# Attention on one core: the weighted values of two steps of the keys issued together

## The reference

```python
attn = jnp.einsum('bhqd,bhkd->bhqk', query, key) / scale
attn = jax.nn.softmax(attn, axis=-1)
out = jnp.einsum('bhqk,bhkd->bhqd', attn, value)
```

## Time and profile before

| | |
|---|---|
| Timed runs, median of 3 | 3951.06 us (3947.47 to 3952.72) |
| Profiled execution, its time by the profiler (its span; the page gives no other) | 4004.2 us |
| Mean granted TensorE clock in it | 0.952 |
| TensorE, VectorE, ScalarE, GpSimd busy in it | 3682.7, 3108.8, 2340.3, 646.8 us |
| Stage that the change touches | 459 to 3400 us of the span |

### The profile page before, as it was taken

One profiled execution on the slowest core, in us unless ns is written; L12 is line 12 of the kernel. 1 busy time (PEld: TensorE's weight loads), 2 busy tenths in 40 slices (PEclk: granted clock), 3 DMA queues, 4 the chain that ended last, 5 costly groups with the idle time before them and its releaser, 6 DMA issues. The chain is left out here.

```text
span 4004.2 us, 70540 instructions
## 1 busy us (share of the span) xinstructions
PE 3682.7 (92%) x19328; PEld 1342.4 (34%) x19328; DVE 3108.8 (78%) x5336; ACT 2340.3 (58%) x4484; POOL 646.8 (16%) x838
## 2 busy tenths in 40 slices
PE   6775999999999999999999999999999999575888
PEld 3432233323323322333233323322332332464555
DVE  6887988888888888888888888888888885575222
ACT  2322477777767776777677767767777777100111
POOL 5554000000000000000000000000000000355554
PEclk9887799999999999999999999999999999776999
DMA  5556202020202111120202020202112000466442
GB/s 152 171 161 170 42 22 50 21 54 13 55 13 57 26 44 38 30 44 24 45 27 54 12 55 12 54 13 59 29 38 44 23 15 15 137 198 190 146 141 85
DMA packets 268209, 258.28 MB, mean 65 GB/s; under 512 B 59140, under 2 KB 225581, under 8 KB 267601
## 3 DMA queue, kind: packets, MB, share of 16 engines
q1 hardware_dynamic: 252496, 224.42, 22.0%
q0 software_dynamic: 15360, 29.50, 2.6%
HBM read 159.56 MB, written 103.49 MB: 66 GB/s over the span
## 5 line engine op out<-in xcount | busy, mean ns | idle before, releaser
L813 DVE TENSOR_REDUCE max_parts<-ps_m 128x1 f32<-128x512 f32 x4096 | 2546.0, 683 | 394.2 <-PE ps_m L698 392.3
L791 ACT ACTIVATE probs<-ps_s 128x512 f32<-128x512 f32 x4096 | 2129.3, 603 | 811.9 <-PE ps_s L718 811.7
L698 PE MATMUL ps_m<-keys,queries 96*128 96x512 bf16 x4096 | 1580.7, 386 | 33.3 <-DMA queries<-split_q 32.9
L718 PE MATMUL ps_s<-queries,keys 99*128 99x512 bf16 x4096 | 1564.4, 383 | 31.5 <-issue 25.4
L733 PE MATMUL ps_o<-probs,vals 128*32 128x512 f32 x8192 | 1094.7, 606 | 0.3 <-ACT weighted L780 0.2
L718 PEld LDWEIGHTS ps_s<-queries,keys 99*128 99x128 bf16 x4096 | 397.1, 97 | 1301.8 <-issue 819.7
L698 PEld LDWEIGHTS ps_m<-keys,queries 96*128 96x128 bf16 x4096 | 400.0, 98 | 474.2 <-DVE max_parts L813 92.5
L659 POOL TENSOR_TENSOR heads_out<-weighted,recip_rows 128x512 f32<-128x512 f32 x64 | 81.3, 1270 | 2103.1 <-DMA recip_rows<-recip_rows_dram 2103.1
L733 PEld LDWEIGHTS ps_o<-probs,vals 128*32 128x32 f32 x8192 | 161.4, 108 | 371.3 <-issue 356.5
L1509 DVE TENSOR_TENSOR hidden<-ps_u,silu 128x320 f32<-128x320 f32 x64 | 30.9, 491 | 178.3 <-PE ps_u L1445 131.3
L647 POOL TENSOR_TENSOR neg_split<-neg_max,zeros_b 128x16 bf16<-128x16 f32 x64 | 14.1, 220 | 771.3 <-DVE neg_max L821 771.3
(11 more groups left out here) (103 smaller groups left out, 1931.7 us busy)
## 6 DMA issues: line engine op xcount, KB each, us to landing
queries<-split_q SPq DMA_DIRECT2D x384, 64.0 KB
rows<-rows_c SPq DMA_DIRECT2D x16, 1032.0 KB, 6.4
vext<-val SPq DMA_DIRECT2D x64, 256.0 KB, 3.6
vals<-vext SPq DMA_DIRECT2D x32, 512.0 KB
recip_rows<-recip_rows_dram SPq DMA_DIRECT2D x64, 256.0 KB
att<-heads_out SPq DMA_DIRECT2D x64, 256.0 KB, 2.7
split_q<-parts SPq DMA_DIRECT2D x96, 128.0 KB
split_k<-parts SPq DMA_DIRECT2D x96, 128.0 KB
```

The costliest lines, as they stand in the source:

```text
L698: pe.matmul(ps_m[bank][:], queries[0:SROWS, par, qt, j, t * P:(t + 1) * P], keys[0:SROWS, par, j, c * 512:(c + 1) * 512], start=True, stop ...
L718: pe.matmul(ps_s[n % BANKS][:], keys[0:MROWS, par, j, k * P:(k + 1) * P], queries[0:MROWS, par, qt, j, :], start=True, stop=True).then_inc ...
L791: act.activation(probs[:, n % RING, :], ps_s[n % BANKS][:], ACT.Exp, scale=SCALE).then_inc(probs_ok[n % BANKS], 1)
L813: dve.tensor_reduce(max_parts[:, lu % 2, g:g + 1], ps_m[bank][:], AX.X, ALU.max).then_inc(maxima_ok[bank], 1)
```

## The change

In `step_of`, the weighted values are no longer issued after every group for the group before, but after every second group (those of even number) for the two groups before: sixteen matmul instructions in a row in place of eight. After group 0 of a step those are the last two groups of the step before, and at the end of the last step two groups are left to weigh instead of one. `weigh`, its waits, the banks and the rings are the same, as is the code of the other engines.

```diff
-                        if n:
-                            weigh(step, n - QUAD)
-                        elif not first:
-                            weigh(step - 1, TILES - QUAD)
+                        if n // QUAD % 2 == 0:
+                            for back in (2 * QUAD, QUAD):
+                                if n:
+                                    weigh(step, n - back)
+                                elif not first:
+                                    weigh(step - 1, TILES - back)
...
-                weigh(STEPS - 1, TILES - QUAD)
+                for back in (2 * QUAD, QUAD):
+                    weigh(STEPS - 1, TILES - back)
```

## The result

The changed kernel takes 4095.99 us (median of 4; 4094.93 to 4098.22) against 3951.89 us (median of 4). The ratio is 1.036, 95% interval 1.035 to 1.038: slower, by 144 us where 182 were forecast (4133 us, range 4075 to 4185).

What follows compares the result with a forecast made beforehand. TensorE was taken to set the pace in attention, VectorE 0.36 us behind per group; units +176, last groups +5 and one more group at the end +1 gave +182 on the 3951 us median: 4133 us, range 4075 to 4185.

Steps and rivals of the forecast that it cites:

- The direction and the mechanism: Attention: slower, as eight tiles in a row outrun VectorE with three ps_m banks; 0.49 us of waiting added per pair.
- from the fourth tile of a run on: Attention runs: the forecast is wrong if TensorE isn't held by reductions from this tile on.
- The saved passage: Between short matmuls and weighted values in attention: one passage in and back less per pair of groups saves 0.175 us.
- Rival A: Attention: drains are the bound and banks don't bind, 5.515 us a pair, 3863 us in all; chance 0.05.
- A pair: Two groups in attention: 6.00 us against 5.69, with a burst of 1.91 us; loses 0.31 us.
- The once-in-a-unit work: Attention, per 16 groups: neg_max +0.44 us, reciprocal +0.16, ps_o copy +0.03 come out; the transposition's 0.29 is swallowed.
- A unit: Sixteen groups in attention: 48.6 us against 45.81, so +2.8 us on each of 62.75 units, +176.
- The last groups: Last 20 groups, without ps_m: TensorE waits for ScalarE; 5.26 us a pair against 4.80, +5 us.
- Rival B: Attention: new waits bring the clock to the lower level a tenth of the time, +256 us, 4389; chance 0.06.
- The row DMAs: DMAs of the maxima in attention: keep their window, costed at nothing; +60 us if they waited in every unit.
- C: Burst in attention: the sixteen matmuls don't run on, 2.00 us instead of 1.91, +45, 4178 us; chance 0.12.
- D: Attention: hidden VectorE work stays hidden or banks free sooner, 0.6 us less a unit, 0.05 a pair, 4070; chance 0.14.

Runs made afterwards that it cites:

- the short reductions: Changed kernel with VectorE reducing only 256 of 512 columns of each ps_m: 3931.2 us, ratio 0.982; the kernel before with the same: 3981.3 us, 0.995.
- the shifted version: Changed kernel with neg_max and the reciprocals moved to the second half of a run: 4117.5 us, ratio 1.042 to the kernel before.
- mended four banks: Changed kernel with four ps_m banks, bank wait and transposition moved to the second scores, ps_o copy moved into the burst: ratio 0.986 to the kernel before.

## Why the prediction was right, and what it had too large

- **The direction and the mechanism**: right. The run of eight waits for reductions from the fifth tile on, tile 7 starts at 3.78 us, VectorE idles 1.09 us in each burst (about 1.2 said). Shown by the short reductions and by two, three and four banks. The sign "from the fourth tile of a run on" in the prediction (and in the first expectation) was a slip against its own sum: the fourth tile has 0.15 us to spare, the fifth is held by 0.02 us and each later one by 0.16.
- **The saved passage**: its size was too small by the terms, and came out right in the total by luck. Rival A's premise, that no bank is late, was wrong. With the wait taken away a pair takes 5.513 us in the loop, A's 5.515; but the burst of sixteen is 0.05 us shorter than A has it, and ScalarE, "ahead of its turn" in the prediction, holds the last scores of each run by about as much. Where ScalarE doesn't, a pair takes 5.45, so one passage less is worth 0.24 us and not 0.175. The trace agrees in so far with the rule that a change of tiling mode drains TensorE (the Trainium skill, TensorEngine Tiling (Array Packing), Key Properties), that a passage in and out has this price; it doesn't show what the engine does in it.
- **A pair**: 5.96 us, not 6.00. The term that was too large is the burst of sixteen, 1.86 and not 1.91 us. The second and third set follow each other closer than the first two, as this timeline of one burst's weight loads and matmuls shows, 0.46 and then 0.43:

```profile
2041.30 1.92 PE L720 MATMUL ps_o<-probs,vals 128*32 128x512 f32 x16
2041.76 0.13 PEld L720 LDWEIGHTS ps_o<-probs,vals 128*32 128x32 f32 x4 [0.30 <-issue]
2042.19 0.13 PEld L720 LDWEIGHTS ps_o<-probs,vals 128*32 128x32 f32 x4 [0.30 <-issue]
2043.16 0.39 PE L705 MATMUL ps_s<-queries,keys 99*128 99x512 bf16 x1
```

  Eight pairs a unit: 0.32 us too much, 20 us over the stage.
- **The once-in-a-unit work**: neg_max +0.35 (0.44 said), reciprocals +0.10 (0.16), copy +0.04 (0.03), transposition swallowed. 0.13 us a unit too much, 8 us in all. The kinds were right, as the shifted version shows.
- **A unit**: 48.18 against 48.6; the difference to the kernel before is 2.37 us, not 2.82. On 62.75 units that is 28 us of the 39 by which the sum for attention (+182, measured +143.5) was too large. This is the term of the sum that was too large, and it is mostly the burst.
- **The pauses between steps**, which I left as they were: the unit with one is 7.8 us longer than the others before (mean of five) and 6.8 after. The written-out first and last steps have units of 48.04. These two are some 7 us more of the 39, and the rest I can't assign. Why the pause is shorter wasn't tried.
- **The last groups**: 5.21 us a pair (5.26 said, 4.80 before), so +4 and not +5, and ScalarE holds TensorE there, as said.
- **The clock**: 0.99 in attention, 1.00 in the last groups, before and after. Rival B's condition, waits inside the run that bring the clock to the lower level, didn't occur, though VectorE now holds TensorE up in every run. The Trainium skill, TensorE: Matmul & The Clock Gate, section on psum-queue depth-cycling, tells of a kernel in which small idle times while cycling through PSUM banks made the clock go up and down. This trace doesn't agree for waits of 0.16 us a tile: the clock stayed at 0.99.
- **The row DMAs**: costed at nothing, and 6.0 us of waits against 10.2 in the whole stage. Right for this change, but with little to spare: runs that shortened the unit or moved the reciprocals made it 33 us (mended four banks) and 68 us (shifted work).
- **C and D**: the burst came out below the forecast, not above, and D's direction is where the measured time lies, 26 us above its 4070: a pair 0.04 us shorter where D has 0.05, and 0.13 us a unit less of uncovered work where D has 0.6. The bank isn't freed sooner, 0.74 us as before.

## What to carry to other kernels

Before work of one engine is gathered into longer bursts, count how many tiles the consumers can take between bursts with the buffers there are: with b banks, a consumer's pace c, a producer's pace p, a delay s from the producer's first step to the consumer's first, and a turn-round r from the start of one consumer step to the refill, tile i (from 0, i at least b) is late as soon as s + (i - b) x c + r exceeds i x p. Here s is 0.42 us, c 0.60, r 0.745 and p 0.44: with three banks tile 3 has 0.15 us to spare and tile 4 is the first that is late, if barely; with four banks tile 7 still has 0.12. A run of four fits three banks and a run of eight needs four, as the pairs of 5.51 and 5.96 us show. The time saved by the longer burst, 0.18 us a pair in the loop with four banks, shrinks to 0.06 with two and is more than lost with three. Then apply the same count to the next consumer: once VectorE no longer held TensorE up, ScalarE did, by 0.05 us. And when a step is shifted to gain a fraction of a us, look at what is queued behind it on the DMA-issuing engine: the shift was worth 28 us by the units' lengths, and the loads issued later cost 49.

## What the runs showed of the hardware that I had not expected

- A burst of float32 matmuls on 32-column strips between bfloat16 matmuls on the full width has the same edges whether it has eight or sixteen instructions: 0.31 us from the last short matmul to it, 0.54 us from its last set of four to the next short one. Inside it the second set starts 0.455 us after the first, and each later one 0.43. Merging two bursts of eight saved 0.24 us where nothing else waited (5.45 against 5.69 us a pair).
- The phases behind attention differ between profiled executions of the same code by up to 98 us, but by session and not at random. From the last group's weighted values to the end they took 589 to 593 us in the four runs of the first session of experiments (kernel before 4004 us), 539 to 544 in the second (3953), 631 to 636 in the third (4042); the DMA engines moved 152, 167 and 142 GB/s there (one run of each). A pair of groups in attention repeats to within a few ns in all three. The profiled execution before has 596 us there and the one after 543, so a difference in span between two profiles must be broken up by stage before it is read as the change's. Why the sessions differ is not known.
